# A four-layer graph network on one core: an X3 edge store a round later, half of the turned copies on VectorE, boundary rows gathered in the last pass, and a quarter of the wide one-hots on ScalarE

## What is computed

```
h = max(layernorm(x), 0);  x = x + L0(h)     # gcn: degree-normed neighbour sum, PReLU
h = max(layernorm(x), 0);  x = x + L1(h)     # weighted neighbour sum, @ W.T + b
h = max(layernorm(x), 0);  x = x + L2(h)     # attention, batch norm over nodes, relu(out + h)
h = max(layernorm(x), 0);  x = x + L3(h)
# L3: edge_attr = relu([h[src], h[dst]] @ W_e + b_e)
#     msg = relu([h[dst], edge_attr] @ W_n1 + b_n1)
#     relu(segment_sum(msg, dst) @ W_n2 + b_n2)
```

## Time and profile before

| what | value |
|---|---|
| median of 3 runs | 2797.51 us (2796.29 to 2801.75) |
| the profiled execution | 2794.54 us, its span 2791.4 us |
| busy over the span: PE, DVE, ACT, POOL | 75%, 69%, 64%, 51% |
| histogram loop | from 34.5 us, last product from 122.2 us |
| X3 pass | about 1745 to 2115 us |
| last pass | about 2115 us to the end |

### The profile page before, as it was taken

One profiled execution on the slowest core, in us unless ns is written; L12 is line 12 of the kernel. 1 busy time (PEld: TensorE's weight loads), 2 busy tenths in 40 slices (PEclk: granted clock), 3 DMA queues, 4 the chain that ended last, 5 costly groups with the idle time before them and its releaser, 6 DMA issues. The chain is left out here.

```text
span 2791.4 us, 52208 instructions
## 1 busy us (share of the span) xinstructions
PE 2086.5 (75%) x11015; PEld 1429.9 (51%) x11015; DVE 1927.7 (69%) x8743; ACT 1785.9 (64%) x4580; POOL 1431.2 (51%) x1442
## 2 busy tenths in 40 slices
PE   3467666666674888848884899566664999999996
PEld 1145444454453777748884444233332666666663
DVE  8878787777874777758885787577774555555552
ACT  0089788878884888859993343799992444444442
POOL 7577777777774666457770000000003566666663
PEclk9789999888987999979997999899996999999998
DMA  3256566556553666647772542699995223232320
GB/s 77 64 162 193 174 184 185 176 170 182 179 171 98 166 169 171 159 140 197 198 197 55 155 126 82 203 307 303 306 308 138 56 76 76 75 82 76 83 72 23
DMA packets 458179, 419.72 MB, mean 150 GB/s; under 512 B 56699, under 2 KB 354574, under 8 KB 458010
## 3 DMA queue, kind: packets, MB, share of 16 engines
q1 hardware_dynamic: 391578, 343.53, 40.8%
q0 software_dynamic: 64192, 74.09, 10.8%
q10 hardware_dynamic: 2240, 0.01, 0.0%
HBM read 236.96 MB, written 184.33 MB: 151 GB/s over the span
## 5 line engine op out<-in xcount | busy, mean ns | idle before, releaser
L2036 POOL DMA_INDIRECT x_bx<-t_X,k_bslot x2 | 2.0, 1016 | 608.2 <-DMA t_X<-k_S 607.9
L2295 POOL DMA_INDIRECT out_dram<-mlp_ou,mlp_iro x200 | 201.4, 1007 | 184.0 <-issue 183.7
L486 POOL DMA_INDIRECT second_xs<-t_X,second_irs x200 | 200.2, 1001 | 124.9 <-issue 51.4
L486 POOL DMA_INDIRECT first_rd<-t_R,a_irs x200 | 202.6, 1013 | 82.5 <-issue 59.4
L2288 POOL DMA_INDIRECT mlp_xs<-t_X,mlp_irs x200 | 203.4, 1017 | 78.0 <-issue 59.7
L486 POOL DMA_INDIRECT a_xs<-in_x_dram,a_irs x200 | 203.4, 1017 | 61.4 <-issue 57.6
L486 POOL DMA_INDIRECT project_xs<-t_X,project_irs x200 | 200.6, 1003 | 63.0 <-issue 58.7
L2348 DVE TENSOR_TENSOR mlp_v<-mlp_ps_r,mlp_b 126x512 f32<-126x512 f32 x50 | 34.6, 691 | 239.8 <-ACT mlp_y L2407 236.5
L2450 PE MATMUL mlp_ps_e<-mlp_h,mlp_we 128*128 128x504 f32 x400 | 188.4, 594 | 1.2 <-ACT mlp_h L2429 1.2
L486 POOL DMA_INDIRECT a_xd<-in_x_dram,a_ird x152 | 161.3, 1061 | 51.9 <-issue 45.4
L2462 PE MATMUL mlp_ps_m<-mlp_e,mlp_wn 128*128 128x504 f32 x400 | 185.3, 586 | 0.0
(11 more groups left out here) (396 smaller groups left out, 6965.5 us busy)
## 6 DMA issues: line engine op xcount, KB each, us to landing
t_X<-first_x SPq DMA_DIRECT2D x194, 256.0 KB, 3.1
first_x<-in_x_dram SPq DMA_DIRECT2D x97, 256.0 KB, 3.8
project_x<-t_X SPq DMA_DIRECT2D x97, 256.0 KB, 3.4
x_x<-t_X SPq DMA_DIRECT2D x97, 256.0 KB, 4.1
t_X<-x_x SPq DMA_DIRECT2D x97, 256.0 KB, 4.7
out_dram<-x_ou SPq DMA_DIRECT2D x97, 256.0 KB, 4.9
t_G<-second_g SPq DMA_DIRECT2D x50, 267.8 KB
t_X<-first_xo SPq DMA_DIRECT2D x50, 252.0 KB
```

The lines of the kernel that those rows point to most:

```text
L486: pool.indirect_dma_start(dst[:, q, :], None, table, bass.IndirectOffsetOnAxis(ap=idx[:, q:q + 1], axis=0)).then_inc(s_rows, 16)
L2295: pool.indirect_dma_start(out, bass.IndirectOffsetOnAxis(ap=iro[s][:, q:q + 1], axis=0), OU[s][:, q, :], None, bounds_check=N - 1, oob_is_ ...
```

## The change

In the histogram pass the fourth wide one-hot of each round is no longer VectorE's: ScalarE forms relu(1 - (i - r)^2) in two instructions, a Square into f32 and a Relu into the f16 tile, with a wait between them. TensorE waits for both engines. VectorE has one small operation more ahead of the loop, the negated row.

In the X3 pass VectorE copies the turned groups with h = 0, ScalarE those with h = 1; the copy is the first thing in VectorE's round. SyncE stores the edge rows of round t - 2 in round t, not those of t - 1. `nbm` is formed at the beginning of the pass. Gather and store of the boundary rows leave the pass.

In the last pass GpSimd gathers the boundary rows first. SyncE first loads the destinations' row and two weights, then stores the boundary rows to a table XB of their own, waits for it, loads the slot rows of rounds 0 and 1 (125 rows from X3, the 126th from XB, so two DMAs for one), and then the other weights. Each round loads slot rows two rounds ahead. The waits for all weights stand at the first instruction that reads one.

```diff
         done(dve.tensor_tensor(rk[:, :], r0[:, :], rk[:, :], ALU.subtract))
+        dve.tensor_scalar(nrk[:, :], rk[:, :], -1.0, None, ALU.mult)
...
-                    dve.tensor_scalar(A[r][:, q, :], ip[:, :], pk[:, k], None, ALU.is_equal)
-                    ins = dve.tensor_scalar(B[r][:, q, :], ir[:, :], rk[:, k], None, ALU.is_equal)
+                    ins = dve.tensor_scalar(A[r][:, q, :], ip[:, :], pk[:, k], None, ALU.is_equal)
+                    if q < GT - 1:
+                        dve.tensor_scalar(B[r][:, q, :], ir[:, :], rk[:, k], None, ALU.is_equal)
                 ins.then_inc(s_one, 1)
...
+        act.wait_ge(s_d, 7)
+        act.wait_ge(s_set, 6)
+
+        def body(t, u):
+            if there(t, NGE):
+                r = u % 2
+                if not before(t, 2):
+                    act.wait_ge(s_pe, t - 1)
+                k = bass.ds(t * GT + GT - 1, 1)
+                act.activation(sq[r][:, :], ir[:, :], ACT.Square, bias=nrk[:, k]).then_inc(s_sq, 1)
+                gate(kp, act, s_sq, t + 1)
+                act.activation(B[r][:, GT - 1, :], sq[r][:, :], ACT.Relu, bias=kp.ones[0:RW, 0:1], scale=-1.0).then_inc(s_oneb, 1)
+
+        steps(act, NGE, 1, 0, body)
         act.wait_ge(s_d, 10)
         act.activation(sd[:, :], c1[:, :], ACT.Sqrt).then_inc(s_sd, 1)
...
                 pe.wait_ge(s_one, t + 1)
+                pe.wait_ge(s_oneb, t + 1)
...
-            ge, se = t - 1, (u - 1) % 4
+            ge, se = t - 2, (u - 2) % 4
             if there(ge, NGE):
                 gate(kp, sp, e_x3, ge + 1)
                 sp.dma_start(erows("X3", ge), kp.rows(ge)).then_inc(e_s3[se], 16)
...
-        sp.wait_ge(s_bx, 64)
-        last = T["X3"][N:ROWS, :].rearrange("(k p) d -> k p d", p=RW)[:, RW - 1, :]
-        for b in range(2):
-            sp.dma_start(last[b * HT:(b + 1) * HT, :], Bx[:, b, :]).then_inc(s_bxs, 16)
-        sp.wait_ge(s_bxs, 32)
-
-    @block.gpsimd
-    def _(pool):
-        for s in range(4):
-            pool.wait_ge(e_s3[s], 16 * len(range(s, NGE, 4)))
-        for b in range(2):
-            pool.indirect_dma_start(Bx[:, b, :], None, T["X3"],
-                                    bass.IndirectOffsetOnAxis(ap=kp.bslot[:, b:b + 1], axis=0)).then_inc(s_bx, 16)
-
...
+        dve.scalar_tensor_tensor(nbm[:, 0:NF], kp.mr2[:, 0:NF, 0], -1.0, kp.mr2[:, 0:NF, 1], ALU.mult, ALU.mult).then_inc(s_nb, 1)
+        dve.scalar_tensor_tensor(nbm[0:TAIL, NF:NF + 1], kp.mr2[0:TAIL, NF:NF + 1, 0], -1.0, kp.mr2[0:TAIL, NF:NF + 1, 1],
+                                 ALU.mult, ALU.mult).then_inc(s_nb, 1)
         done(dve.tensor_tensor(v(10, 2), kp.bn[:, 0:2], kp.bn[:, 2:4], ALU.add))
...
+        def turned(g, s):
+            if there(g, XG):
+                dve.wait_ge(s_t, g + 1)
+                if not before(g, 2):
+                    dve.wait_ge(s_o, g - 1)
+                dve.tensor_copy(feat(HTb[s % 2], g), featps(psT[s % 2], g)).then_inc(s_hd, 1)
+
         def body(t, u):
             g2, u2 = t - 2, (u - 2) % 4
+            turned(2 * (t - 1), 2 * ((u - 1) % 4))
             if there(t, NGE):
                 dve.tensor_tensor(kp.rows(t), kp.rows(t), Sb[0:RW, :, :], ALU.mult).then_inc(e_v0, 1)
...
-                turned(2 * (t - 1) + h, 2 * u1 + h)
+                if h == 1:
+                    turned(2 * (t - 1) + h, 2 * u1 + h)
...
-                    pe.wait_ge(s_h, g - 1)
+                    pe.wait_ge((s_hd, s_h)[s % 2], t)
...
-                pe.wait_ge(s_h, g + 1)
+                pe.wait_ge((s_hd, s_h)[s % 2], t + 1)
...
+        def load(t, u):
+            if there(t, NGE):
+                if not before(t, 8):
+                    sp.wait_ge(s_o, t - 7)
+                sp.dma_start(Xd[u][0:RW - 1, :, :], state_rows(T["X3"])[0:RW - 1, bass.ds(t * GT, GT), :]).then_inc(s_xd[u], 16)
+                sp.dma_start(Xd[u][RW - 1:RW, :, :], T["XB"].rearrange("(a k) d -> a k d", a=1)[:, bass.ds(t * GT, GT), :]).then_inc(s_xd[u], 16)
+
+        def rows(t, u):
+            if there(t, NGE):
+                r = u % 2
+                if not before(t, 2):
+                    sp.wait_ge(s_sel, t - 1)
+                sp.dma_start(dr[r][:, :].rearrange("p (k j) -> p k j", k=GT),
+                             T["dr"][bass.ds(t * GT, GT), :].partition_broadcast(RW)).then_inc(s_dr[r], 16)
+
+        rows(0, 0)
         sp.dma_start(we[:, :, :], a["L3_gnn_W_e"].rearrange("(k p) n -> p k n", p=128)).then_inc(s_w, 16)
         sp.dma_start(wn1[:, :, :], a["L3_gnn_W_n1"].rearrange("(k p) n -> p k n", p=128)).then_inc(s_w, 16)
+        sp.wait_ge(kp.s_bound, 64)
+        for b in range(2):
+            sp.dma_start(T["XB"][b * HT:(b + 1) * HT, :], Bx[:, b, :]).then_inc(s_bxs, 16)
+        sp.wait_ge(s_bxs, 32)
+        load(0, 0)
+        load(1, 1)
...
+            load(t + 2, (u + 2) % 8)
+            rows(t + 1, (u + 1) % 8)
...
+        for b in range(2):
+            pool.indirect_dma_start(Bx[:, b, :], None, T["X3"],
+                                    bass.IndirectOffsetOnAxis(ap=kp.bslot[:, b:b + 1], axis=0)).then_inc(kp.s_bound, 16)
+
...
-            dve.wait_ge(s_xd[v], landed(t, v, 8))
+            dve.wait_ge(s_xd[v], landed(t, v, 8, 2))
...
-        dve.wait_ge(s_w, 16 * (7 + GT))
...
+                if before(g, 1):
+                    dve.wait_ge(s_w, 16 * (7 + GT))
...
+                if h == 0 and before(g, 1):
+                    act.wait_ge(s_w, 16 * (7 + GT))
...
-        pe.wait_ge(s_w, 16 * (7 + GT))
...
+            if h == 0 and before(g, 1):
+                pe.wait_ge(s_w, 16 * (7 + GT))
```

More of the change, by code:

```diff
@@ L506, in phase_hist @@
     B = [sb(f"b{i}", [RW, GT, NC], F16) for i in range(2)]
+    nrk = sb("nrk", [RW, NT])
+    sq = [sb(f"sq{i}", [RW, NC]) for i in range(2)]
     cnt = sb("cnt", [128, NC])
@@ L519, in phase_hist @@
                                                   sem("root"), sem("rtable_stored"))
+    s_sq, s_oneb = sem("squared"), sem("one_hot_by_scalar")
     D = [sb(f"d{j}", [RW, GT, 128]) for j in range(NX)]
@@ L1947, in phase_x3 @@
     s_x, s_z = m.ring("x2_loaded", 8), sem("norm")
-    s_t, s_h, s_o, s_r, s_b = sem("turned"), sem("relu"), sem("product"), sem("biased"), sem("back")
+    s_t, s_h, s_hd, s_o, s_r, s_b = sem("turned"), sem("relu"), sem("relu_by_vector"), sem("product"), sem("biased"), sem("back")
     s_x3, s_out = sem("x3"), sem("out")
@@ L2073, in _ @@
         done(dve.tensor_tensor(wd[:, :], wg2[:, :], kp.ident[:, :], ALU.add))
-        dve.scalar_tensor_tensor(nbm[:, 0:NF], kp.mr2[:, 0:NF, 0], -1.0, kp.mr2[:, 0:NF, 1], ALU.mult, ALU.mult).then_inc(s_nb, 1)
-        dve.scalar_tensor_tensor(nbm[0:TAIL, NF:NF + 1], kp.mr2[0:TAIL, NF:NF + 1, 0], -1.0, kp.mr2[0:TAIL, NF:NF + 1, 1],
-                                 ALU.mult, ALU.mult).then_inc(s_nb, 1)
         def total(g, s):
@@ L2175, in _, with turn @@
         pe.wait_ge(s_c, 12)
-        def turn(g, s):
+        def turn(g, s, t):
             if there(g, XG):
@@ L2185, in turn, with product @@
                 ins.then_inc(s_t, 1)
-        def product(g, s):
+        def product(g, s, t):
             if there(g, XG):
-                pe.wait_ge(s_h, g + 1)
+                pe.wait_ge((s_hd, s_h)[s % 2], t + 1)
                 if not before(g, 2):
@@ L2207, in body @@
                 back(2 * (t - 2) + h, 2 * u2 + h)
-                product(2 * (t - 1) + h, 2 * u1 + h)
-                turn(2 * t + h, 2 * u + h)
+                product(2 * (t - 1) + h, 2 * u1 + h, t - 1)
+                turn(2 * t + h, 2 * u + h, t)
         steps(pe, NGE, 3, 2, body)
@@ L2239, in phase_mlp @@
     b2 = sb("b2", [128, GT, 128])
+    Bx = sb("bx", [HT, 2, 128])
     psH = [m.ps(f"h{i}", [128, 512]) for i in range(2)]
@@ L2246, in phase_mlp @@
     s_w, s_idx, s_rows, s_xd = sem("weights"), sem("idx_ready"), kp.s_gathered, m.ring("state_loaded", 8)
+    s_bxs = sem("bound_stored")
     s_dr, s_sel = m.ring("drow_loaded", 2), sem("select")
@@ L2267, in body @@
         def body(t, u):
-            if there(t, NGE):
-                if not before(t, 8):
-                    sp.wait_ge(s_o, t - 7)
-                sp.dma_start(Xd[u][:, :, :], state_rows(T["X3"])[:, bass.ds(t * GT, GT), :]).then_inc(s_xd[u], 16)
-                r = u % 2
-                if not before(t, 2):
-                    sp.wait_ge(s_sel, t - 1)
-                sp.dma_start(dr[r][:, :].rearrange("p (k j) -> p k j", k=GT),
-                             T["dr"][bass.ds(t * GT, GT), :].partition_broadcast(RW)).then_inc(s_dr[r], 16)
+            load(t + 2, (u + 2) % 8)
+            rows(t + 1, (u + 1) % 8)
         steps(sp, NGE, 1, 0, body, 8)
@@ L2516, in gnn_kernel @@
         ("R", (N, 2)), ("X1", (ROWS, D)), ("X2", (ROWS, D)), ("G", (SLOTS, GW)), ("X3", (ROWS, D)),
[L2517 removed]
+        ("GE", (SLOTS, D)), ("dr", (NT, RW)), ("XD", (NX * GT * RW, D)), ("XB", (NT, D)), ("B8", (NT, SW)))}
     with ExitStack() as whole:
```

4 lines of the change are left out of this document (removed).

## The result

| | kernel before | change |
|---|---|---|
| median | 2797.93 us (2796.29 to 2801.75, 4 runs) | 2780.66 us (2775.94 to 2782.06, 4 runs) |
| profiled execution, its span | 2794.54, 2791.4 us | 2780.05, 2778.5 us |

The ratio is 0.9937, 95% interval 0.9925 to 0.9949: 17.3 us less (14 to 21), where 26.3 were forecast. The time lies in the range, 10 us above the forecast.

What follows compares the result with a forecast made beforehand. VectorE was taken to bound the histogram, ScalarE X3, TensorE the last pass. Histogram 11.1, X3's beginning 0.7, its rounds 5.5 and seam 9 made 26.3 us off 2794.5; with 3.0 added for the median, 2771 us, range 2755 to 2783.

Steps and rivals of the forecast that it cites:

- with its gathers x = 1.33 + 0.15x / 1.31 gives 1.50: Histogram: VectorE's round without one wide one-hot takes 1.33 us, and gathers stretching one-hots by 0.15 each make it 1.50.
- The second pace: Histogram: two buffers tie VectorE's and TensorE's rounds and hand-overs together, 1.55 us a round at the lower clock, 1.2 at the upper.
- GpSimd's gathers end about 117 us, before the loop's tail even when that tail comes 11 us earlier: Histogram's end: GpSimd's gather list would not hold the pass, even with the loop's tail 11 us earlier.
- the second circle: X3 rounds: loop through VectorE's copy, the product, ScalarE's bias and next norm, over two rounds; 13.22 us, 6.61 a round.
- The first circle: X3 rounds: one-round loop from VectorE's copy through product, turn, total and edge steps back to the copy; 6.48 us.
- times 47 rounds in full swing: X3 rounds: 6.60 us against 6.71 in each of 47 rounds, 5.2 us of the 5.5 forecast.
- the third rival: X3 slower: at the lower clock the circle grows about 1 us a round; whole 2799 to 2825 us; chance 0.04.
- boundary store 4.1 behind it: Seam, inside the last pass: the boundary rows' store follows their gather by 4.1 us, part of 3.5 us gained there.
- the weights, loaded later, are needed only about 10 us behind the statistics: Last pass: weights loaded later are needed only about 10 us behind the first statistics.
- X3 freed fully: Rival: looser circles let X3's round fall to 6.25 us, 16 us more gain, 2751 to 2760 us; chance 0.17.
- the seam keeps its length: Rival: slot rows still land late, seam gives 4 to 5 us, histogram 8; whole 2776 to 2784 us; chance 0.17.
- the DMA floor: X3 rounds: the DMA engines' share allows no round under 6.25 us; the skill's limit gives 5.8.

Runs made afterwards that it cites:

- p_less: The change with one of the histogram pass's twelve own-row sets read by four plain DMAs instead of four gathers; 2773.98 us, ratio 0.9923 to the kernel before.
- b_again: The kernel before, unchanged, run once more for a second profile; 2798.24 us.
- b_plain: The kernel before with its 12 gathers of own rows taken off GpSimd and x's first rows loaded by plain DMAs instead; 2795.49 us, one run.
- c_early: The change with VectorE's copy of the turned group moved right behind the totals of its own round; 2752.64 us, ratio 0.9849 to the kernel before.
- best: The change with c_early's copy move and the two large weights loaded behind the slot rows of rounds 0 and 1; 3375.25 us, ratio 0.9854, on a slower chip.

## Why the time came out 10 us above the prediction

The direction and the range held, but three terms were mis-sized, the histogram's 3.1 us too small, those of X3's rounds and of the seam 3.5 and 3.2 too large, and a fourth, what other passes give back, was missing (4.3). That the first covers part of the others is luck.

**Histogram, forecast -11.1, measured -14.2.** The failed step is "with its gathers x = 1.33 + 0.15x / 1.31 gives 1.50". It lets every gather stretch a one-hot, as in the rows of before; in the change the gathers keep to a place in the round where none starts 0.6 to 0.7 us behind them, and the round is the bare 1.33 (measured 1.34). The second pace that I set against it (1.55 at the lower clock) hardly occurs: the granted clock is 1.00 in this stretch, where it was 0.87. By the loop alone the term would be 20.3 us. The second failed step is "GpSimd's gathers end about 117 us, before the loop's tail even when that tail comes 11 us earlier": true of an 11 us gain, not of 20; then the pass ends some 6 us behind the last gather's issue, and with one set of gathers less (p_less) 4.7 us earlier. ScalarE's cover was read right in its price (0.62 us each, the pair 1.24, 1.34 with its waits), but it left no room: at 1.34 ScalarE is as near to being the bound as VectorE. The Trainium skill's rule (ScalarE: Activation LUTs, Rules for kernel authors), VectorE being up to about three times faster an element, agrees in its direction, 0.62 against 0.31 us an operation, a factor of two. The change pays because ScalarE was idle; one more one-hot moved there would have made it the bound, by an estimate of two pairs at 1.24 us against VectorE's 1.34 (no run tried it).

**X3, the beginning: -0.7 forecast.** Last attention row to first norm: 18.1, 18.6 and 18.8 us in before, b_again and b_plain, 17.9, 18.0 and 17.6 in after, p_less and c_early. The 0.7 is there; the wait now ends at `x_wd`.

**X3, the rounds, forecast -5.5, measured -2.0.** The circle was the right one: ScalarE waits for the product behind VectorE's copy, and the pace has the period of two rounds that the second circle has. It is 13.33 us long from the copy at 1892.75 to that at 1906.08, not 13.22: copy to product 0.81 (I read 0.72), product to bias 1.25 (1.17), norm to turn 1.69 (1.78). The first circle holds the shorter of two rounds, 6.62 from 1892.75 to 1899.37 and not 6.48: its product to turn is 0.96, not 0.9. Steady rounds fell from 6.71 to 6.66 on the mean of some 40 in each trace, half of the 0.11 forecast. The other failed step is "times 47 rounds in full swing", which prices every round at the full clock. Where TensorE's clock falls for a product, such a round took 7.6 to 7.7 us before (five in the profiled execution) and takes 8.1 to 8.2 now (four), since ScalarE's norm no longer lies beside the product: the third rival in small, some 0.6 us a round on top of the 1.0 that it cost before. That takes back most of what the steady rounds give, so that forty rounds gained 0.5 us where 4.4 were forecast; the 2.0 measured are mostly the shorter start of X3, which no term of the prediction has. The rival's mechanism is real, its frequency was too low to make the whole slower.

**The seam, forecast -9.** The earlier release is right (5.5 forecast, 5.0 measured). The -3.5 inside the last pass became +1.1 in the profiled pair (statistics 15.4 us behind the first DMA for 14.3) and about -0.3 on the mean of all executions (14.6 for 14.9). The failed step is "boundary store 4.1 behind it": it was 7.7 here, 5.75 to 7.7 in the four executions. The 4.1 us taken for the slot rows were nearly right (2110.44 to 2115.39, 4.95), and so were the 2.4 for the store (2.0). The prediction looked for what lies ahead of the slot rows, and missed that the 888 KB of SyncE's first three loads are issued around the gather that the slot rows wait for. The three executions with the weights behind show the price: gather to store falls from 6.7 to 4.1 us on the mean, and the statistics come 1.6 us earlier, since the sources' gathers then land last. Over all executions the seam gives 5.8 us.

**What was given back.** 14.2 + 0.7 + 2.0 + 5.8 = 22.7 us; the medians differ by 17.3. From the first pass's start to attention's last row, code that the change doesn't touch, three executions without it took 1605.7, 1606.4 and 1610.8 us, three with it 1612.3, 1608.6 and 1608.8: 2.3 us more on the mean, the ranges overlapping. They part better by when the first pass starts: 1605.7 and 1606.4 where it starts at 137 to 138 us, 1608.6 to 1612.3 in the four, b_plain among them, where it starts at 119 to 131. By b_again's own measure (within 1 us) something is given back for an earlier start; why, no run shows, and two executions on one side are few. The last pass behind its first statistics took 646.7 to 647.2 and 648.3 to 649.7: 2.0 more. These two close the sum to 18.4.

The traces show where those 2.0 us lie. From VectorE's first `mlp_v` to its last the pass takes 590.5 us in before and after alike; the loss is in the first rounds:

```profile
2129.26 0.87 DVE L2350 TENSOR_SCALAR k_S<-mlp_dr,k_dcol 126x126 f32<-126x126 f32 x4 [5.74 <-DMA mlp_dr<-t_dr]
...
2132.67 0.33 PE L2534 MATMUL mlp_ps_h<-k_ident,mlp_z 126*128 126x126 f32 x1 [2.17 <-DVE mlp_z L2395]
```

VectorE waits 5.7 us for the destinations' row of round 1 (5.7 in c_early, 7.2 in p_less, no such wait before the change), and TensorE 2.2 us for the norm behind it. The change issues this row behind nine loads of weights and biases and the slot rows of round 2, and the prediction's "the weights, loaded later, are needed only about 10 us behind the statistics" left out what else they are now ahead of. c_early and best have the same wait; no run moves the row forward.

**The rivals.** X3 freed fully is what c_early does, at 6.23 us a round as priced (6.25); the change didn't get there because the circles were real. "VectorE's idleness is inside the circle" stands. That the seam keeps its length nearly happened; the histogram beyond its bound made up for it. On the DMA floor, the row-made estimate (0.93 x 6.71 = 6.25 us) fits: at 6.24 the share is 1.00 to 1.02, though ScalarE's own work ends there too, so that no run shows the floor by itself. The Trainium skill's limit of about 358 GB/s (DMA: Bandwidth & Descriptors, Where 436 GB/s comes from) is not reached here: with the engines full they moved 331 to 336 GB/s, so by their share the 5.8 us a round estimated from it would have been too low.

## What to carry to other kernels

When an operation goes to an engine with room, its place in that engine's list matters more than the room: the same copy gave 2 us of X3 at the head of the next round and 29 (335.7 to 306.3) behind the two additions of its own, so close every circle through the new place, over as many rounds as the buffers span, before choosing it. When a loop gets faster, ask of every other engine in the pass how long its own list is, since the barrier waits for the longest. When loads are reordered, list everything that now stands behind them, not only what they carry. Before a small transfer that others wait for, put nothing large in the queues, not even in another engine's.
